# A 64-step attention on one core: weight tiles transposed in 32x32 blocks by VectorE instead of 128x128 by TensorE

## The reference, cut to what matters

```python
q = jnp.einsum('bsd,ed->bse', x, Wq).reshape(bsz, seqlen, HQ, D)      # x: 8 batches x 128 rows x 512, HQ = 32, D = 128
k = jnp.einsum('bsd,ed->bse', x, Wk).reshape(bsz, seqlen, HK, D)      # HK = 8
v = jnp.einsum('bsd,ed->bse', x, Wv).reshape(bsz, seqlen, HK, D)
...
probs = jax.nn.softmax(scores, axis=-1)                                # 512 cached keys and 128 own
o = jnp.einsum('bhqk,bkhd->bqhd', probs, v_all)
return jnp.einsum('bse,de->bsd', o, Wo)
```

## Time and profile before

| | |
|---|---|
| median of 3 runs | 1564.07 us (1563.36 to 1565.45) |
| profiled execution, its own time | 1554.2 us |
| span of the profile | 1552.5 us |
| mean granted TensorE clock | 0.991 of full speed |
| TensorE busy | 1509.9 us, 97% |
| VectorE busy | 1180.2 us, 76% |
| ScalarE busy | 893.2 us, 58% |
| GpSimd busy | 879.2 us, 57% |

### The profile page before, as it was taken

How to read it: one execution, slowest core, us unless ns; L and a number is a source line. 1 busy time by engine, 2 the same in 40 slices (tenths; PEclk the granted TensorE clock), 3 DMA queues, 4 the chain that set the end, 5 groups by cost and what they waited for, 6 DMA issues and landing times.

```text
span 1552.5 us, 27376 instructions
## 1 busy us (share of the span) xinstructions
PE 1509.9 (97%) x8984; PEld 1293.2 (83%) x8984; DVE 1180.2 (76%) x2668; ACT 893.2 (58%) x2308; POOL 879.2 (57%) x1231
## 2 busy tenths in 40 slices
PE   6899999989999999999999999999999999999997
PEld 4788888778888888888888888888888888888885
DVE  3666665767888888888888878888887888777865
ACT  2433333356666666666666666666666666666641
POOL 1111234236667666766676676667666766676521
PEclk8999999999999999999999999999999999999999
DMA  6654555322222222222222222222222222311102
GB/s 209 209 161 134 148 165 162 77 82 70 69 71 73 69 71 61 76 70 70 64 72 71 71 66 70 70 71 72 70 72 66 70 69 65 89 59 48 42 27 82
DMA packets 74085, 133.39 MB, mean 86 GB/s; under 512 B 17426, under 2 KB 27026, under 8 KB 73946
## 3 DMA queue, kind: packets, MB, share of 16 engines
q1 hardware_dynamic: 56482, 97.56, 21.2%
q0 software_dynamic: 16464, 33.85, 7.5%
q10 hardware_dynamic: 1000, 0.23, 0.1%
HBM read 107.47 MB, written 7.34 MB: 74 GB/s over the span
## 4 chain that ended last, share of the span: by engine, by line
PE 91%; DVE 3%; ACT 2%; issue 2%; POOL 1%; DMA 1%; ACTq 0%; POOLq 0%; DVEq 0%; SPq 0%
PE ps_t L948 15%; PE ps_o L739 11%; PE ps_o L741 10%; PE ps_o L740 10%; PE ps_b L739 5%; PE ps_b L741 5%; PE ps_b L740 5%; PE ps_q L741 4%; PE ps_q L740 4%; PE ps_q L739 4%; PE ps_t L762 3%; PE ps_a L739 3%; PE ps_a L793 3%; PE ps_a L741 3%; PE ps_a L740 3%
## 5 line engine op out<-in xcount | busy, mean ns | idle before, releaser
L1443 ACT ACTIVATE sm<-sm,mn 128x640 f32<-128x640 f32 x256 | 211.4, 826 | 234.5 <-DVE mn L1912 234.5
L1788 DVE TENSOR_TENSOR pT_lo<-ps_t,pT_hi 128x512 fp32r<-128x512 f32 x320 | 220.2, 688 | 113.5 <-ACT pT_hi L1366 113.3
L622 POOL DMA_INDIRECT kraw<-in_L_cond_k_cache_dram,idx_a x200 | 197.5, 988 | 89.1 <-issue 74.3
L1366 ACT ACTIVATE pT_hi<-ps_t 128x512 fp32r<-128x512 f32 x320 | 188.5, 589 | 84.7 <-PE ps_t L948 84.7
L622 POOL DMA_INDIRECT vraw<-in_L_cond_v_cache_dram,idx_a x200 | 198.7, 994 | 59.6 <-issue 59.3
L948 PE MATMUL ps_t<-ident,sm 128*128 128x128 f32 x1280 | 195.7, 275 | 3.2 <-ACT sm L1453 1.5
L948 PEld LDWEIGHTS ps_t<-ident,sm 128*128 128x128 f32 x1280 | 147.9, 140 | 51.4 <-DVE qT_lo L1788 17.9
L639 POOL TENSOR_TENSOR z<-pairs_p,zl 128x128 f32<-128x128 f32 x160 | 57.9, 402 | 206.8 <-DVE pairs_p L1652 206.8
L739 PE MATMUL ps_o<-pT_lo,v_hi 128*128 128x512 f32 x320 | 129.8, 406 | 0.0
L741 PE MATMUL ps_o<-pT_hi,v_hi 128*128 128x512 f32 x320 | 125.5, 392 | 0.0
L740 PE MATMUL ps_o<-pT_hi,v_lo 128*128 128x512 f32 x320 | 124.9, 390 | 0.0
(11 more groups left out here) (257 smaller groups left out, 4370.1 us busy)
## 6 DMA issues: line engine op xcount, KB each, us to landing
fv<-st SPq DMA_DIRECT2D x128, 128.0 KB, 2.3
tab<-tab_scratch SPq DMA_DIRECT2D x64, 256.0 KB
wraw<-n_L_attn_weight_qkv_dram SPq DMA_DIRECT2D x8, 1536.0 KB, 7.3
wpraw<-_L_attn_weight_proj_dram SPq DMA_DIRECT2D x8, 1024.0 KB, 9.4
mask<-mask_scratch SPq DMA_DIRECT2D x64, 128.0 KB
wtile<-in_L_cond_Wq_dram SPq DMA_DIRECT2D x28, 256.0 KB
wtile<-in_L_cond_Wo_dram SPq DMA_DIRECT2D x28, 256.0 KB
kraw<-in_L_cond_k_cache_dram,idx_a POOLq DMA_INDIRECT x200, 2.6
```

Source lines behind the costliest of these rows:

```text
L622: pool.indirect_dma_start(raw[:, par, c, :], None, rows_d, bass.IndirectOffsetOnAxis(idx[:, k:k + 1].bitcast(U32), 0)).then_inc(arrived[pa ...
L1366: act.activation(dst, src, ACT.Copy).then_inc(t_hi, 1)
L1443: act.activation(sm[:, h, :], sm[:, h, :], ACT.Exp, bias=mn[:, h:h + 1], scale=-1.0, accum_out=den[:, h:h + 1]).then_inc(e_done, 1)
L1788: dve.tensor_tensor(lo, src, hi.bitcast(F32), ALU.subtract).then_inc(t_lo, 1)
```

## The change

A weight tile of the second attention is loaded in 128-byte pieces: four transfers of 32 partitions each, 512 pieces apiece, so that the 128x128 transpose across blocks of 32 is done by where the pieces land. VectorE then transposes the sixteen 32x32 blocks with one instruction per tile (STREAM_TRANSPOSE) from `wtile` into `wa_turn` or `wo_turn`, which share their memory with the low parts. ScalarE rounds that copy into the high part, now from SBUF, and VectorE subtracts in place and so makes the low part. TensorE and its banks `ps_t` have no part in it any more, and the ring has seven groups in each step. Wo's rows are put into another order by this (row 4m + c of Wo in column 128c + m of the output product); the weights of the last layer are therefore read with a stride of four elements (`late_group`). Wo's four tiles for group 0 (`w0_tail`) still go through TensorE and get the same order by reads of PSUM with a stride of four.

```diff
@@ -483,7 +491,13 @@
-                sp.dma_start(wtile[:, slot, :], src).then_inc(wt_in[slot], 16)
+                if t < 6:
+                    blocks = src.rearrange("(j b) (c i a) -> i b c j a", j=4, c=NC_, i=4)
+                else:
+                    blocks = src.rearrange("(b j) (c i a) -> i b j c a", j=4, c=NC_, i=4)
+                for i in range(4):
+                    sp.dma_start(wtile[32 * i:32 * i + 32, slot, :].rearrange("b (u v a) -> b u v a", u=4, v=4),
+                                 blocks[i]).then_inc(wt_in[slot], 16)
@@ -528,14 +542,12 @@
-                        wait_alone(sp, t_full, base + t_index(n, name, last)[0] + 1)
+                        wait_alone(sp, wt_turned, g * TILES_W + t + 1)
                         load_wtile(g + 1, t + 2, t % 2)
@@ -948,10 +960,6 @@
-            def w_tile(idx, bank, t, arrivals):
-                pe.wait_ge(wt_in[t % 2], arrivals)
-                transposed(idx, bank, [(c, wtile[:, t % 2, c * P:(c + 1) * P]) for c in range(NC_)])
@@ -1047,13 +1055,13 @@
-                    transposed(i, bank, [(c, wbraw[:, t, c * P:(c + 1) * P]) for c in range(NC_)])
+                    transposed(i, bank, [(c, wbraw[:, t, c:HID:NC_]) for c in range(NC_)])
@@ -1120,7 +1125,7 @@
-                        pe.wait_ge(t_lo, base + t_index(6, "W9", last)[0] + 1 + 2)
+                        pe.wait_ge(wt_lo, (g + 1) * TILES_W)
@@ -1412,6 +1419,12 @@
+            def turned_hi(g, t):
+
+                act.wait_ge(wt_turned, g * TILES_W + t + 1)
+                act.activation(w_dst(wa_hi, wo_hi, (g + 1) % 2, t),
+                               w_dst(wa_turn, wo_turn, (g + 1) % 2, t), ACT.Copy).then_inc(wt_hi, 1)
@@ -1885,7 +1905,24 @@
+                def turn(t):
+
+                    dve.wait_ge(wt_in[t % 2], (g * (TILES_W // 2) + t // 2 + 1) * 64)
+                    raw = wtile[:, t % 2, :]
+                    if t < 6:
+                        raw = raw.rearrange("p (c m) -> p c m", c=NC_)
+                    else:
+                        raw = raw.rearrange("p (j c a) -> p c j a", j=4, c=NC_)
+                    dve.transpose(w_dst(wa_turn, wo_turn, (g + 1) % 2, t), raw).then_inc(wt_turned, 1)
+
+                def turned_low(t):
+                    dve.wait_ge(wt_hi, g * TILES_W + t + 1)
+                    dve.tensor_tensor(w_dst(wa_lo, wo_lo, (g + 1) % 2, t), w_dst(wa_turn, wo_turn, (g + 1) % 2, t),
+                                      w_dst(wa_hi, wo_hi, (g + 1) % 2, t).bitcast(F32),
+                                      ALU.subtract).then_inc(wt_lo, 1)
```

More of the change, by code:

```diff
@@ L340, in groups_of, with tiles_of @@
         def groups_of(n, last):
+            w = []
             if last:
                 w = [f"L{i}" for i in range(7) if i // 2 + 1 == n] + [f"Y{i}" for i in range(2) if N - 2 + i == n]
-            else:
-                w = [f"W{W_FIRST[n] + i}" for i in range(W_COUNT[n])] if W_COUNT[n] else []
             nxt = not (last and n == N - 1)
             return w + ["K"] * nxt + ["D0", "D1", "D2"] + ["q"] * nxt + ["D3", "DS"]
+        def tiles_of(n, last):
+            return [W_FIRST[n] + i for i in range(W_COUNT[n])] if W_COUNT[n] and not last else []
         PER_G = sum(len(groups_of(n, False)) for n in range(N))
@@ L530, in step @@
                     load_wtile(g + 1, 1, 1)
[L531 to L534 removed]
+                for t in tiles_of(n, last):
+                    if t + 2 < TILES_W:
+                        wait_alone(sp, wt_turned, g * TILES_W + t + 1)
                         load_wtile(g + 1, t + 2, t % 2)
[L536 to L538 removed]
+                    elif g + 2 < G:
+                        wait_alone(sp, wt_turned, g * TILES_W + t + 1)
                         load_wtile(g + 2, t + 2 - TILES_W, t % 2)
@@ L1453, in normalise @@
                     act.activation(sm[:, h, :], sm[:, h, :], ACT.Copy, scale=rd[:, h:h + 1]).then_inc(p_act, 1)
-                w = [m for m in names if m[0] in "WLY"]
+                w = [m for m in names if m[0] in "LY"]
+                tiles = tiles_of(n, last)
                 exponentials(0)
@@ L1458, in step @@
                     group(w[0])
+                if tiles:
+                    turned_hi(g, tiles[0])
                 exponentials(1)
@@ L1461, in step @@
                     group(w[1])
+                if len(tiles) > 1:
+                    turned_hi(g, tiles[1])
                 if not first:
@@ L1931, in step @@
                     group(w[0])
+                if tiles:
+                    turn(tiles[0])
                 normalise(0)
@@ L1935, in step @@
                     group(w[1])
+                if len(tiles) > 1:
+                    turn(tiles[1])
                 if not (first and n < 1):
@@ L1940, in step @@
                 group("D0")
+                if tiles:
+                    turned_low(tiles[0])
                 least(2)
@@ L1961, in step @@
                     add_output(J, (n - 1) % N, first)
+                if len(tiles) > 1:
+                    turned_low(tiles[1])
                 group("DS")
```

20 lines of the change are left out of this document (13 added, 7 removed).

## The result

| | before | after |
|---|---|---|
| median, each taken in turn with the other | 1563.46 us (1560.09 to 1565.45, 7 runs) | 1569.23 us (1567.59 to 1570.69, 7 runs) |
| profiled execution, its span | 1554.2, 1552.5 us | 1567.59, 1565.8 us |

The ratio is 1.0036, 95% interval 1.0025 to 1.0048: the changed kernel is a little slower, as forecast (1569.0). The two profiled executions differ by 13.4 us though, the medians by 5.8; most of what follows is about this difference.

A forecast was written before the change was run, and what follows sets the result against it. TensorE, 97% busy, was taken to set the pace. Tile steps +2.8 us, strided loads +1.5 and the first tile +0.5 made +4.8; with 9.9 us from profiled execution to median, 1569 us, range 1557 to 1612.

The forecast's parts named there:

- The chain of a two-tile step: VectorE and ScalarE alternate up to least(2), 2.00 late less 0.50 slack; each two-tile step 0.60 us longer, 12.6 over 21.
- One-tile steps: In one-tile steps least(2) is 0.60 late, 0.10 paid, 0.45 saved: each 0.35 us shorter, 9.8 over 28.
- the subtraction stays, from SBUF, 0.68 us by the nearest row of two SBUF operands: VectorE's subtraction for a tile's low part takes 0.68 us from SBUF, as from PSUM.
- D0 as ever: In a one-tile step D0 on ScalarE stays at 8.36 because it waits for TensorE's transposes.
- I add the same to both: The timed median lies 9.9 us above the profiled execution, before and after: 1559 profiled, 1569 median.
- Pieces: The 128-byte transfers of weight tiles take at most 28 ns each, 3.6 us for 128 per engine, and stay hidden.
- The 7.2 us a tile: Estimate for a tile's transfer if each piece under 512 bytes counts as two rows of 28 ns; still hidden.
- The first tile: Its load in step 0 may be late once by 0 to 5 us; taken as +0.5 us.
- Strided loads: The last layer's six groups of strided transposes have weight loads of 209 ns against 140; taken as +1.5 us.
- Cheap transposes (0.43): Rival: VectorE's transpose takes 0.43 us instead of 0.69, 10.9 us less in two-tile steps, 1558; chance 0.13.
- dear ones (1.38): Rival: VectorE's transpose takes twice 0.69 us, adding 42.9 us in all, 1612; chance 0.15 with what lies above.
- TensorE as the bound: Rival: with another 1.5 us of cover in the chain, 31.5 - 2 us come through, 1535; chance 0.08.

The follow-up runs named there:

- E1: Changed kernel with ScalarE's two copies of the turned tiles moved behind the copy of D0: 1551.21 us, ratio 0.9878 to the kernel before.
- E11: Changed kernel with every tile transposed twice by VectorE: 1609.22 us.
- E9: Changed kernel with ScalarE's tile copies behind D0, pieces kept, and GpSimd's gathers of values spread out: 1584.74 us, ratio 1.0200 to the kernel before.
- E3: Changed kernel with each tile loaded by one transfer in rows of 2 KB, its weights permuted: 1562.17 us, ratio 0.9951 to the kernel before.
- C: The kernel before, unchanged, timed again as a control: 1564.43 us, its profiled execution 1567.15.
- a set like the last: The third set of experiments, E8 to E11, on one chip; the kernel before took 1554.01 us in it.
- E4: Changed kernel with the last layer's weights read in contiguous columns instead of strided: 1569.17 us, ratio 0.9998 to the kernel before.
- E6: Changed kernel with ScalarE's two copies behind D0 and tiles loaded in whole rows of 2 KB: 1536.82 us, ratio 0.9828 to the kernel before.
- E5: The kernel before with its tiles loaded in 128-byte pieces and nothing else changed: 1566.92 us, ratio 1.0009.
- the second set: The experiments from C through E6, with one more, on one chip; the kernel before took 1564.73 us in it.
- E10: Changed kernel with transposes, copies and low parts late, pieces kept, GpSimd's gathers spread: 1552.34 us, ratio 0.9991 to the kernel before.
- E2: Changed kernel with ScalarE's copies, VectorE's transposes and the low parts all moved late: 1577.73 us, ratio 1.0054 to the kernel before.
- E8: The kernel before with GpSimd's four gathers of values spread around the statistics of k and q: 1581.46 us, ratio 1.0176.

## Why the prediction came out as it did

**The chain of a two-tile step: right, its total partly by luck.** Every point of it was met within 0.1 us in the step shown, and E1 and E11 test it from both sides. Forecast over 21 steps +12.6; measured against the first profile +11.4 (n = 3 and 5: +7.2, n = 1: +4.1). But the typical step isn't 0.60 longer. At n = 3 and 5 it is 0.43 (medians 18.45 and 18.88), at n = 1 it is 0.88 (18.48 and 19.36): there TensorE waits at a second place, which the sum didn't have, for VectorE's low part of q ahead of DS, and takes up DS 0.51 us behind the own-key transposes instead of 0.16.

**One-tile steps: the path right, the size wrong.** Forecast 0.35 shorter each, 9.8 us; measured 17.94 on average against 18.03, 2.4 us. least(2) stood at 9.93 instead of 9.56: D0's signal 0.14 late with pieces in flight, and the subtraction 0.20 longer beside GpSimd's. The step that failed is "the subtraction stays, from SBUF, 0.68 us by the nearest row of two SBUF operands" (the other half, D0's signal, by "D0 as ever"): 0.68 alone, up to 1.02 here and 1.76 in E9, where GpSimd subtracts in SBUF at the same time. Moving an operand from PSUM to SBUF was costed by its length alone. The Trainium skill states this rule (SBUF — State Buffer, Who interferes with whom): a VectorE instruction with two SBUF inputs contends with a GpSimd instruction that reads SBUF, and which of the two blocks is decided by the order of issue. The rows of E3 and of E9 agree, with either engine as the loser.

**"I add the same to both": wrong.** The 9.9 us between the first profile and the median were taken for a constant. By C they were held signals, 11.3 us there. In the trace of the changed kernel the same signal is rarely held: it is on time in 49 of 51 recorded cases. It falls due at other moments, within 0.50 us of a gather's start in 46 of them, where none is held and where C held none either. ScalarE's waits for held signals are 1.1 us in the profile, and its profiled execution is 1.6 below the median, not 9.9. So the forecast of 1559 for a profiled execution was 8.6 too low, the 9.9 added to it 8.3 too much, and 1569 came out right by two errors that cancel, which is luck. The difference between the medians, 5.8, is then what the chain costs less the held signals that the new order is spared. In a set like the last, where before takes 1554.0, the changed kernel might lose more; it wasn't run there.

**Pieces: hidden, with a price elsewhere.** They were to take at most 28 ns each. Queue 1 in the 5.5 us around one tile's landing:

```profile
q1 hardware_dynamic: 2112, 0.26, 30.7%
```

30.7% of 16 engines over 5.5 us is 27.0 engine-us for 2112 packets, 12.8 ns each; no tile came late. The Trainium skill (DMA: Bandwidth & Descriptors, Specifications) says that below 512 bytes a transfer becomes a read-modify-write and misses the line rate. The loss of rate is seen: in E3, the same 0.26 MB in whole rows takes 17.1% of 16 engines over 6 us (813 to 819), 16.4 engine-us against 27.0. Whether anything is read back no row shows. The 7.2 us a tile estimated from it is not borne out: 27.0 engine-us are 1.7 us of 16 engines. SP's issues take 637 ns each instead of 333, in its waits. What they cost in the changed kernel, 7.0 us by E3, is paid in D0's later signals and in the longer subtractions behind them; why pieces delay that signal isn't known.

**The small terms.** The first tile wasn't late. Strided loads were 0.3 us, forecast 1.5. The last group is 1.6 longer than in the first profile, with 1.3 in its steps n = 3 and 4 that neither E3 nor E4 takes away; the steps without a tile gave 1.3, and the second attention begins 1.7 later. Of the 1.3, 1.1 is the one held signal that ScalarE waited for, at n = 7 of group 1 (18.66). The causes of the others are open.

**The rivals.** Cheap transposes (0.43) and dear ones (1.38) fell with 0.704. TensorE as the bound fell in this order of work, but E1 and E6 show that it was one move away: it takes the copies out of ScalarE's first half.

**Open.** What holds TensorE's signals. In C and E5 they come 1.70 to 1.80 us after the start of a gather of GpSimd, but the first profile of before has signals due at the same moments and none held. They also go by the order of work: of the second set, C has 25 in 45 recorded signals and E6 one in 43. The only attempt to part them from the gathers met a set in which before took 1554.0, its time without any. E6 is the fastest kernel here, but its weights are permuted; of those that leave the computation whole, E1 is the one clearly faster than before, ratio 0.9878. E10's order without its side effect would be worth, by its own steps, some 27 us less than 1552 (seven first steps of 20.0 to 24.4 against 17.9 and, in the last group, 19.8), an estimate that wasn't run.

## What to carry to other kernels

When a step moves from a well-covered engine to two engines that must alternate, count the alternations: here the work was 0.7 us per tile, and the wait came from transpose, copy, other work, transpose, copy standing in one line. Put what nobody waits for soon (a copy for the next group) behind what somebody does.

Before an operand is moved from PSUM to SBUF on VectorE, look at what GpSimd does at that moment; E11 adds that a delay can push another of VectorE's instructions into it. And one profiled execution that is several microseconds faster than the timed runs is not a scaled copy of them: find the wait that it lacks before building a sum on it.

## What the runs showed of the hardware that I had not expected

- TensorE's signal can come 1.5 us late (E2; up to 2.0 in E1) while its later instructions run on; two signals are then released 0.06 us apart. At the copy of the new keys and values, the place followed here, it was released within 2.1 us after the start of a gather. In C all 25 signals due 1.02 to 1.70 us after that start were held to 1.70 to 1.77.
- Two subtractions from SBUF on VectorE and GpSimd hold each other up: 0.68 became 1.76 us behind one of 1.29 (E9). A division on VectorE became 0.94 instead of 0.57 beside GpSimd's rounding (E11).
- After a stand of 3.45 us TensorE's granted clock was 0.50 of full speed for 6.8 us (E8), which with the same wait made a step 1.3 us longer.
- A transpose of 128x512 four-byte elements in 32x32 blocks takes 704 ns, about as long as an ordinary instruction of that width (0.68 to 0.69), and hardly varies (697 to 710 ns in 70 cases).
- A 128-byte piece takes 12.8 ns of a DMA engine, and the issue of 512 of them 637 ns of SP's queue against 333 for 128 rows.
